# One turn of a six-layer attention stack: a copy and a mask less on ScalarE, the token shift in three parts, half of a reduction folded on GpSimd

## The reference

```
for i in range(6):
    x = attn_layer(shift_tokens(x), Wqkv[i], q_scale[i], k_scale[i], Wo[i]) + x
    x = ffn_layer(shift_tokens(x), ln_g[i], ln_b[i], W1[i], b1[i], W2[i], b2[i]) + x

attn_layer: q, k, v = split(x @ Wqkv)             # 16 heads of 64
            q = l2norm(q) * qs;  k = l2norm(k) * ksc   # norm over the 64 of a head
            rotary turn of q and k, causal softmax(8 q k^T) within 32 tokens, times v, times Wo
ffn_layer:  xn = (x - mean) / sqrt(var + 1e-5) * g + b
            a, gate = split(xn @ W1 + b1);  return a * gelu(gate) @ W2 + b2
shift_tokens: channels 64..127 come from the token before
```

## Time and profile before

| | |
|---|---|
| median of 3 runs | 2848.09 us (2845.32 to 2854.91) |
| the profiled execution: its time, its span | 2847.98 us, 2846.2 us |
| TensorE busy | 2691.9 us, 95% of the span |
| VectorE busy | 2600.1 us, 91% |
| ScalarE busy | 2246.7 us, 79% |
| GpSimd busy | 2116.7 us, 74% |
| mean granted TensorE clock | 0.988 of full speed |
| conditioning block | about the first 391 us |

### The profile page before, as it was taken

One profiled execution on the slowest core, in us unless ns is written; L12 is line 12 of the kernel. 1 busy time (PEld: TensorE's weight loads), 2 busy tenths in 40 slices (PEclk: granted clock), 3 DMA queues, 4 the chain that ended last, 5 costly groups with the idle time before them and its releaser, 6 DMA issues.

```text
span 2846.2 us, 92826 instructions
## 1 busy us (share of the span) xinstructions
PE 2691.9 (95%) x36416; PEld 2060.1 (72%) x36417; DVE 2600.1 (91%) x3375; ACT 2246.7 (79%) x3776; POOL 2116.7 (74%) x1529
## 2 busy tenths in 40 slices
PE   8799978999999999999999999999999999999996
PEld 7577756777777777777777777777777777777774
DVE  7899968999999999999999999999999999999993
ACT  5799957878788787878888787888878787887873
POOL 6766658777778777778777787777787777877771
PEclk9899999999999999999999999999999999999998
DMA  1000013232223332223232232222322322322222
GB/s 57 24 2 2 1 35 76 67 76 69 67 69 75 73 73 66 69 71 75 66 79 69 66 75 71 72 67 70 76 67 68 79 62 68 72 67 58 64 66 79
DMA packets 103719, 178.41 MB, mean 63 GB/s; under 512 B 29350, under 2 KB 52708, under 8 KB 103396
## 3 DMA queue, kind: packets, MB, share of 16 engines
q1 hardware_dynamic: 102372, 174.60, 25.2%
q10 hardware_dynamic: 1152, 1.20, 0.1%
HBM read 22.62 MB, written 2.10 MB: 9 GB/s over the span
## 4 chain that ended last, share of the span: by engine, by line
PE 30%; POOL 16%; issue 15%; ACT 11%; DMA 7%; DVE 5%; SPq 1%; POOLq 0%; ACTq 0%; DVEq 0%
PE pa L843 9%; POOL spare L1446 8%; DMA kT<-spare 7%; PE px L872 5%; PE pg L982 3%; PE ps L903 3%; PE pg L960 3%; PE px L917 3%; PE pg L974 2%; POOL xs_lo L1432 2%; DVE ss L1269 2%; ACT spare L1095 2%; POOL pr L1484 2%; ACT spare L1041 1%; POOL spare L1455 1%
## 5 line engine op out<-in xcount | busy, mean ns | idle before, releaser
L1446 POOL TENSOR_TENSOR spare<-spare,qk_t 128x1024 f32<-128x1024 f32 x384 | 910.1, 2392 | 10.9 <-POOL xs_lo L1432 8.1
L843 PE MATMUL pa<-w_hi,xs_hi 128*128 128x512 f32 x1152 | 511.9, 444 | 25.3 <-issue 8.6
L1462 POOL TENSOR_TENSOR sm<-sm,inv 128x512 f32<-128x512 f32 x192 | 201.8, 1051 | 429.2 <-DVE sm L1307 361.4
L1285 DVE TENSOR_TENSOR qk_t<-pa,rot 128x1024 f32<-128x1024 f32 x384 | 464.6, 1210 | 1.6 <-ACT spare L1048 0.8
L1276 DVE TENSOR_TENSOR spare<-pa,rot 128x1024 f32<-128x1024 f32 x384 | 464.6, 1210 | 0.0
L1269 DVE TENSOR_REDUCE ss<-spare 128x16 f32<-128x1024 f32 x384 | 457.7, 1192 | 6.1 <-ACT spare L1041 5.2
L843 PE MATMUL pa<-w_hi,xs_lo 128*128 128x512 f32 x1152 | 459.2, 399 | 0.3 <-DMA pT<-prT 0.3
L843 PE MATMUL pa<-w_lo,xs_hi 128*128 128x512 f32 x1152 | 455.0, 395 | 0.0
L872 PE MATMUL px<-ident_sb,spare 128*128 128x128 f32 x3072 | 407.2, 276 | 18.8 <-POOL spare L1455 11.9
L1455 POOL TENSOR_TENSOR spare<-spare,inv 128x1024 f32<-128x1024 f32 x192 | 365.9, 1905 | 69.6 <-ACT inv L1080 65.3
L872 PEld LDWEIGHTS px<-ident_sb,spare 128*128 128x128 f32 x3072 | 340.4, 140 | 105.1 <-issue 44.6
(11 more groups left out here) (178 smaller groups left out, 5926.1 us busy)
## 6 DMA issues: line engine op xcount, KB each, us to landing
kT<-spare SPq DMA_DIRECT2D x384, 256.0 KB, 3.7
pT<-prT SPq DMA_DIRECT2D x768, 64.0 KB, 2.0
w_part<-in_Wqkv SPq DMA_DIRECT2D x40, 192.0 KB, 3.7
wo<-in_Wo SPq DMA_DIRECT2D x6, 512.0 KB, 5.5
c_h<-in_x SPq DMA_DIRECT2D x4, 512.0 KB, 9.5
spare<-in_x SPq DMA_DIRECT2D x8, 256.0 KB, 4.8
out<-spare SPq DMA_DIRECT2D x8, 256.0 KB, 2.5
wo<-in_W SPq DMA_DIRECT2D x6, 341.0 KB, 5.2
```

What stands on the lines that cost most here:

```text
L843: last = pe.matmul(pa[(u + c) % 2][:, half * 512:half * 512 + 512], x[:, j * P:(j + 1) * P], w[:, at], start=(k == 0), stop=(k == 2))
L1285: dve.tensor_tensor(halves(qk_t[:, c, :]), halves(pa[(3 * j + c) % 2][:])[:, :, ::-1, :], table.unsqueeze(1).to_broadcast([P, HEADS, 2, DH ...
L1446: pool.tensor_tensor(qk_r[:, c, :], qk_r[:, c, :], qk_t[:, c, :], ALU.add)\
```

## The change

- ScalarE makes no copy `fc` of the centred values. The variance goes into the bank `ps` of the scores instead of `pg`, so that the centred values stay in `pg`; the inverse deviation goes to `fr` in SBUF; VectorE's `normalise` multiplies `pg` by g and by `fr` in one instruction.
- As `ps` holds the variance for a while, ScalarE leaves out the mask of turn 0, and TensorE writes it by a matmul of the identity with the mask (both bfloat16) at the head of `scores` in turn 1, after the logarithm has been taken. The waits for masks are renumbered.
- TensorE's `variance` moves from between `transpose_k` and `project_v` into the middle of turn 0's `project_v`, between its two halves, and waits for VectorE's subtraction in that turn.
- The shift is in parts of 256, 128 and 128 tokens: ScalarE does them in turns 2, 3 and 0, GpSimd in turns 3, 3 and 0.
- GpSimd adds the upper half of every head of k's squares to the lower (`fold_squares_k`, at the head of every turn), and VectorE sums only 32 columns a head. q's squares are summed as before.
- VectorE sums q's squares before it turns the probabilities, and takes the reciprocal of the denominators after `rest_of_outputs` in turns 0 to 2.

```diff
-        HALF_TOK = 2 * P
+        SHIFT_PART = ((0, 2 * P), (2 * P, P), (3 * P, P))
@@ TensorE, project
                     for half in range(2):
+                        if between and half == 1:
+                            between()
@@ TensorE, project_q
-                        if j % 2 == 0:
-                            pe.wait_ge(s["xs_ready"], 4 * i + j + 2)
+                        if j != 1:
+                            pe.wait_ge(s["xs_ready"], 6 * i + (2 if j == 0 else 2 * j))
@@ TensorE, project_v
-                        project(i, j, 2, "v_full", l, None if isinstance(n, int) else lambda: await_probs(n - back, back))
+                        project(i, j, 2, "v_full", l, None if isinstance(n, int) else lambda: await_probs(n - back, back),
+                                (lambda: variance(i, 2)) if j == 0 else None)
+                    elif j == 0:
+                        variance(i, 2)
@@ TensorE, scores
+                        if j_now == 1:
+                            pe.wait_ge(s["sub_done"], n)
+                            if group(i, 2)[1]:
+                                pe.wait_ge(s["fln_done"], group(i, 2)[0] + 1)
+                        if j_now == 1 or isinstance(n, int) and n == 0:
                             pe.matmul(ps[:], ident_b[:], mask_b[:], start=True, stop=False, skip_group_check=True)
-                        wait_for(pe, s["masked"], n)
+                        else:
+                            pe.wait_ge(s["masked"], {0: i * 3 - 1, 2: i * 3, 3: i * 3 + 1}[j_now])
@@ TensorE, variance
                         pe.wait_ge(s["fsq_ready"], g + 1)
-                        pe.wait_ge(s["fc_ready"], g + 1)
-                        pe.matmul(pg[:], mean[:], fx[:], start=True, stop=True).then_inc(s["var_done"], 1)
+                        pe.wait_ge(s["sub_done"], min(i * GT - 1, NT) if isinstance(i, int) else i * GT - 1)
+                        pe.matmul(ps[:], mean[:], fx[:], start=True, stop=True).then_inc(s["var_done"], 1)
@@ TensorE, body
-                        if j == 0:
-                            variance(i, 2)
@@ ScalarE
-                        act.activation(fc[:], pg[:], ACT.Identity, scale=ln_par[:, 0:1]).then_inc(s["fc_ready"], 1)
-                        act.activation(fx[:], pg[:], ACT.Ln, bias=eps_c[:]).then_inc(s["fln_done"], 1)
+                        act.activation(fx[:], ps[:], ACT.Ln, bias=eps_c[:]).then_inc(s["fln_done"], 1)
-                        act.activation(pg[:], fx[:], ACT.Exp, scale=-0.5).then_inc(s["frs_ready"], 1)
+                        act.activation(fr[:], fx[:], ACT.Exp, scale=-0.5).then_inc(s["frs_ready"], 1)
@@ ScalarE, body
-                            copy_centred(i, 2)
                         if j == 0:
-                            shift_hi(i, 0, 1)
-                        if j == 2:
-                            shift_hi(i, -1, 0)
+                            shift_hi(i, 0, 2)
+                        if j >= 2:
+                            shift_hi(i, -1, j - 2)
-                        write_mask(i, j, 1)
+                        if j > 0:
+                            write_mask(i, j, 1)
@@ VectorE
+                def sum_squares_k(i, j, back):
+                    n, j, live = tile(i, j, back)
+                    if live:
+                        dve.wait_ge(s["folded_k"], n + 1)
+                        wait_for(dve, s["floored"], n)
+                        dve.reduce_sum(ss[:, 1, :], heads(sq)[:, :, 0:DH // 2], AX.X).then_inc(s["sum_k"], 1)
-                        dve.wait_ge(s["fc_ready"], g + 1)
+                        dve.wait_ge(s["ffn_loaded"], (g // GROUPS + 1) * FFN_DMAS * 16)
                         dve.wait_ge(s["frs_ready"], g + 1)
-                        dve.tensor_tensor(pg[:], fc[:], pg[:], ALU.mult).then_inc(s["fn_mul"], 1)
+                        dve.scalar_tensor_tensor(pg[:], pg[:], ln_par[:, 0:1], fr[:], ALU.mult, ALU.mult)\
+                            .then_inc(s["fn_mul"], 1)
@@ VectorE, body
                         maximum(i, j, 2)
+                        sum_squares_q(i, j, 0)
                         turn_probs(i, j, 3)
-                        sum_squares(i, j, 0, 0, "sq_q", "sum_q")
...
                         denominators(i, j, 2)
+                        if j == 3:
+                            reciprocals(i, j, 2)
                         rest_of_outputs(i, j, 3)
+                        if j < 3:
+                            reciprocals(i, j, 2)
@@ GpSimd
+                def fold_squares_k(i, j, back):
+                    n, j, live = tile(i, j, back)
+                    if live:
+                        pool.wait_ge(s["sq_k"], n + 1)
+                        low, high = heads(sq)[:, :, 0:DH // 2], heads(sq)[:, :, DH // 2:DH]
+                        pool.tensor_tensor(low, low, high, ALU.add).then_inc(s["folded_k"], 1)
@@ GpSimd, body
                     for j in range(GT):
+                        fold_squares_k(i, j, 0)
                         norm_scores(i, j, 2)
...
                         if j == 0:
-                            shift_lo(i, 0, 1)
+                            shift_lo(i, 0, 2)
+                        if j == 3:
+                            shift_lo(i, -1, 1)
```

More of the change, by code:

```diff
@@ L654, in stack @@
         fs = sb("fs", [DM, GTOK])
[L655 removed]
+        fr = sb("fr", [DM, GTOK])
         fx = sb("fx", [DM, GTOK])
@@ L829, in await_probs, with project @@
                         pe.wait_ge(s["oT_lo_ready"], n)
-                def project(i, j, c, full, l, before_last=None):
+                def project(i, j, c, full, l, before_last=None, between=None):
                     u = 3 * j
@@ L890, in transpose_k, with scores @@
                         transposes(j, 1, "tk_done")
-                def scores(i, j, back):
-                    n, j, live = tile(i, j, back)
+                def scores(i, j_now, back):
+                    n, j, live = tile(i, j_now, back)
                     if live:
-                        if isinstance(n, int) and n == 0:
+                        if j_now == 1:
[3 more added lines that the diff above has]
+                        if j_now == 1 or isinstance(n, int) and n == 0:
                             pe.matmul(ps[:], ident_b[:], mask_b[:], start=True, stop=False, skip_group_check=True)
-                        wait_for(pe, s["masked"], n)
+                        else:
+                            pe.wait_ge(s["masked"], {0: i * 3 - 1, 2: i * 3, 3: i * 3 + 1}[j_now])
                         pe.wait_ge(s["tq_out"], n + 1)
@@ L1133, in tables, with shift_hi @@
                         act.preload_act_table_set(name)
-                def shift_hi(i, back, half, first=False):
+                def shift_hi(i, back, part, first=False):
                     g, live = group(i, back)
@@ L1138, in shift_hi @@
                     if live:
-                        at = bass.ds((g % GROUPS) * GTOK + half * HALF_TOK, HALF_TOK)
-                        to = slice(half * HALF_TOK, (half + 1) * HALF_TOK)
+                        first_tok, toks = SHIFT_PART[part]
+                        at = bass.ds((g % GROUPS) * GTOK + first_tok, toks)
+                        to = slice(first_tok, first_tok + toks)
                         act.wait_ge(s["res_ready"], g + 1)
-                        wait_for(act, s["v_full"], g * GT - 2 * (1 - half))
+                        wait_for(act, s["v_full"], g * GT - (2 - part))
                         act.copy(xs_hi[0:64, to], res[0:64, at]).then_inc(s["xs_hi_ready"], 1)
@@ L1314, in denominators, with reciprocals @@
                         dve.reduce_sum(den[:], keys(pr[:]), AX.X).then_inc(s["den_done"], 1)
+                def reciprocals(i, j, back):
+                    n, j, live = tile(i, j, back)
+                    if live:
                         dve.wait_ge(s["den_done"], n + 1)
@@ L1424, in _, with shift_lo @@
             def _(pool):
-                def shift_lo(i, back, half, first=False):
+                def shift_lo(i, back, part, first=False):
                     g, live = group(i, back)
@@ L1428, in shift_lo @@
                     if live:
-                        at = bass.ds((g % GROUPS) * GTOK + half * HALF_TOK, HALF_TOK)
-                        to = slice(half * HALF_TOK, (half + 1) * HALF_TOK)
-                        chunk = 2 * g + half
+                        first_tok, toks = SHIFT_PART[part]
+                        at = bass.ds((g % GROUPS) * GTOK + first_tok, toks)
+                        to = slice(first_tok, first_tok + toks)
+                        chunk = 3 * g + part
                         rest = lambda dst, src: pool.tensor_tensor(dst, src, hi, ALU.subtract)
@@ L1530, in _ @@
                 shift_lo(0, 0, 1, True)
+                shift_lo(0, 0, 2, True)
                 pool.wait_ge(first_loaded, 3 * 16)
```

20 lines of the change are left out of this document (8 added, 12 removed).

## The result

The changed kernel takes 2877.93 us (median of 4, 2876.50 to 2879.28) against 2850.10 us for the kernel before (4 runs): a ratio of 1.0092 with a 95% interval of 1.0077 to 1.0108, slower. The forecast was 2868 us, within a range of 2830 to 2884. The profiled execution has a span of 2874.8 us against 2846.2.

A forecast was written before the change was run, and what follows sets the result against it. TensorE was taken as the bound, with only its waits to win back. 30 plain rounds x 0.6, plus 16 x 0.15, minus 0.6, gave +19.8 us on 2847.98: 2868 us, range 2830 to 2884 (own range 2856 to 2884).

The forecast's parts named there:

- the second rival: Gain and loss cancel: only one of three late events reaches TensorE, at 0.1 or so; within 8 us of 2848; chance 0.21.
- The first rival: Keys' wait before turn 1's scores shrinks and nothing gives it back: 16 us off, 2832 us; chance 0.27.
- The bound: TensorE, busy 48.08 of a 49.37 us round, has about 1.3 us to give back; other savings only shorten its waits.
- ScalarE up to the keys' copy: Turn 0, copy left out and shift halved: of 0.8 us saved, the keys' DMA starts 0.4 us earlier.
- The variance inside the projection of v: Turn 0: TensorE newly waits 0.45 us for q's sine; logarithm 0.76 late, GELU 0.4, second gate block 0.25.
- Scores of turn 1: TensorE writes the mask, then starts turn 1's scores at 1542.75 against 1542.99: 0.25 us gained, lost again at the gate.
- VectorE: Saving of 0.5 us a turn worth nothing; probabilities turned later, so TensorE about 0.5 late at turn 1's last v matmul.
- GpSimd: Fold taken as 1.2 us; late `norm_keys` makes TensorE 0.6 to 0.85 late at turn 2's transposes of k.
- the plain round: One of 30 rounds without weight rounding: 0.6 us longer at the fold's low bound, 0.85 at the high.
- Rounds with weight rounding: 16 longer rounds in which a layer's weights are rounded: +0.15 us each, between -0.3 and +0.6.
- the three late events: GELU, probabilities' DMA and keys' norm; the rival where gain and loss cancel lets only one reach TensorE, at 0.1 or so.
- the third: GpSimd bounds turns 1 and 0: fold at 1.6 us or more, `norm_keys` over 1 us late; 2894 us; chance 0.08.

The follow-up runs named there:

- The variance behind v: The changed kernel with the variance after all of turn 0's v instead of between its halves: ratio 1.0260 to the kernel before, plain round 51.32 us.
- the runs on the kernel before: Among them, the kernel before with the shift in parts of 256, 128 and 128: 0.9982; with the last part in turn 2: 0.9983; denominators also later: 0.9987.

## Why the prediction was right

The forecast of 2868 us was 10 us short, and its own range, 2856 to 2884, holds the 2877.93. The stated range of 2830 to 2884 says less, as it also holds the second rival and most of the first. What speaks for the prediction is that the waits came where it had put them.

*The bound.* Right: only TensorE's waits can be won back. They were worth 1.3 us a round at most, and no kernel here won 0.1 of them in a plain round.

*ScalarE up to the keys' copy.* The copy of k started 0.39 us earlier, 0.4 was said. It is lost in the 1.15 us for which ScalarE stands ahead of the logarithm, and with the last shift part in turn 2 the logarithm is no earlier either.

*The variance inside the projection of v.* Right in place and size: TensorE idle 0.54 us ahead of v (0.45 said), the variance at 1538.35 (1538.35), the logarithm at 1539.41 (1539.45), the GELU at 1546.60 (1546.6), the second gate block 0.18 late (0.25). What this costs was put too low: with the slower start behind the wait TensorE is 0.41 us late at the next transposes. With fold and order undone, which leaves this event alone, the round is 0.39 longer. The variance behind v shows that a further delay of the logarithm carries to the round whole.

*Scores of turn 1.* 1542.75 was said, 1542.91 came: the gain was 0.08 us and not 0.25. It changes nothing, as the gate hung on ScalarE.

*VectorE.* The turning of turn 1 started at 1546.59 (1546.55 said), and v's last matmul was 0.55 us late (0.5 said). The split was wrong: 0.39 came from the gate, where 0.25 was said, and 0.16 from the DMA. The sum for the DMA's landing gives 1551.10 and not 1551.15. That VectorE's saving is worth nothing agrees with the changed kernel, where VectorE waits 0.5 us a round for ScalarE right behind it (L1354: 5.4 us in 10 times), but no run has the saving without the fold. The reason given was too simple in any case: the runs on the kernel before show that VectorE's `rest_of_outputs` stands right behind the keys' wait. And the cost of the new order was charged against it alone, though with the fold the old order is 0.2 us a round worse.

*GpSimd.* The fold took 1.29 us, the high bound, and `norm_keys` ended at 1574.02 - 14.12 = 1559.90, just the high end of 1559.65 + 0.25. The transposes of k in turn 2 were 0.77 late, within the 0.6 to 0.85 said. The prediction's own figures give less: 1559.4 + 0.25 and 1559.65 + 0.25 are 0.46 and 0.71 behind 1559.19. In turn 0 the fold was said to end with the subtraction; it held `norm_scores` there by 0.5 us (1552.81 - 14.12 = 1538.69, against 1538.16), which no matmul waited for.

**The term that was mis-sized is the plain round: +0.6 was taken, the low end, and it measured +0.77 (50.15 against 49.38).** The reason given, that a late TensorE gives the others time, was an argument without a row; the sum with the high end, 0.85, would have given 7.5 us more, 2875. Rounds with weight rounding were put at +0.15. Summed over the profiled executions, the 30 plain rounds take 1501.7 us against 1479.6, 0.74 more each, and the 16 others 811.8 against 807.1, 0.29 more each. That is 26.8 of the 28.6 us between the spans; the forecast's terms for the same rounds were 18 and 2.4 us. The other 1.8 us lie before the first and behind the last of these rounds, where the forecast had -0.6.

The first rival failed at its own condition: ScalarE was 0.4 us late behind the mask left out, where less than 0.25 was its condition. The second needed two of the three late events to stay away from TensorE, and all three came. GpSimd, the third, did become the last of the late events in turn 2, but at 0.77 and not at 1.0.

## What to carry to other kernels

Where an instruction lies over a wait of its engine, it costs nothing, and moving it can cost twice: once where the wait is laid bare, and once in everything that needed its result. Here the bare wait, 0.54 us, was paid for by the keys' wait that went away; the late result was not. Before work is taken off an engine, look where its next wait for another engine is: what is saved ahead of that wait is not saved. When several engines are within tenths of a microsecond of each other, late events replace each other instead of adding, so that undoing parts one at a time misprices them; count of each only what it adds to the delay that is already there. And a wait costs more than the late start of its first matmul: here 0.18 us at the start had become 0.41 by the next transposes.

## What was not expected of the hardware

An addition in place on GpSimd, both halves read from one tile in runs of 32 columns at a stride of 64, costs what two full inputs cost: 1.285 us on average for 512 columns over the 192 of them in the page, where the line through the contiguous 384- and 1024-column rows gives 1.29. So neither the stride between the runs nor working in place cost anything to be seen. An exponential of ScalarE that reads what the logarithm just before it wrote starts 0.73 us after it (1553.53 to 1554.26), where an instruction that does not depend on it starts after 0.58: 0.15 us more with the dependence; the follower was the copy of the mask in the one case and the exponential in the other.
